# First stage of an adaLN transformer block: the blocks of normalized x transposed by a trip through memory and by VectorE

## The reference, cut to what matters

```python
# x (4, 1024, 1024) f32; wq (1024,1024), wk, wv (1024,256), wo (1024,1024); c (4,1024), wmod (1024, 6*1024)
mod = (_silu(c) @ wmod).reshape(4, 6, 1, -1)
sa, ca, ga, sb, cb, gb = (mod[:, n] for n in range(6))
ga, gb = (sign(g) * maximum(abs(g), 0.25) for g in (ga, gb))
h = _layernorm(x) * (1 + ca) + sa
q = h @ wq + bq; k = h @ wk + bk; v = h @ wv + bv      # 32 query heads, 8 key/value heads of 32
x = x + ga * (softmax(q k^T / sqrt(32)) v @ wo + bo)
h = _layernorm(x) * (1 + cb) + sb
x = x + gb * mixture_of_4_lora_experts(h)               # top 2 of 4, rank 16
```

## Time and profile before

| | us |
|---|---|
| median of 3 runs | 2806.36 (2805.2 to 2808.12) |
| the profiled execution, its own time | 2811.7 |
| its span | 2809.9 |
| block 1 / block 2 of the first stage | 69.64 / 74.06 |
| start of block 0's group 4 / of block 1 / of block 7 | 63.94 / 123.73 / 554.97 |

### The profile page before, as it was taken

One profiled execution on the slowest core, in us unless ns is written; L12 is line 12 of the kernel. 1 busy time (PEld: TensorE's weight loads), 2 busy tenths in 40 slices (PEclk: granted clock), 3 DMA queues, 4 the chain that ended last, 5 costly groups with the idle time before them and its releaser, 6 DMA issues.

```text
span 2809.9 us, 48988 instructions
## 1 busy us (share of the span) xinstructions
PE 2757.9 (98%) x14654; PEld 1701.5 (61%) x14654; DVE 2181.6 (78%) x2801; ACT 1529.6 (54%) x2963; POOL 1908.4 (68%) x710
## 2 busy tenths in 40 slices
PE   7999999999999999999999999999999999999998
PEld 4788888884444444444444444444444447888886
DVE  4433434348999999999999999999999968667665
ACT  3111111116776767777777776776767754545543
POOL 2433333317999999999999999999999985111110
PEclk9999999999999999999999999999999999999998
DMA  7544443434434344344444433444444443333231
GB/s 263 182 143 136 144 140 132 136 115 136 91 87 100 85 87 99 87 90 94 94 91 89 96 88 87 96 90 90 90 98 90 91 130 102 107 113 105 98 112 68
DMA packets 167501, 307.05 MB, mean 109 GB/s; under 512 B 49985, under 2 KB 91393, under 8 KB 159361
## 3 DMA queue, kind: packets, MB, share of 16 engines
q1 hardware_dynamic: 158352, 240.05, 29.3%
q0 software_dynamic: 9072, 66.06, 11.5%
HBM read 159.12 MB, written 79.82 MB: 85 GB/s over the span
## 4 chain that ended last, share of the span: by engine, by line
PE 74%; DVE 2%; ACT 1%; issue 1%; POOL 0%; DVEq 0%; ACTq 0%; POOLq 0%
PE back_ps L1348 21%; PE back_ps L1362 18%; PE s_ps L1322 16%; PE s_ps L1838 12%; PE back_ps L1887 2%; PE back_ps L1379 2%; PE back_ps L1859 1%; PE back_ps L1906 1%; DVE mx L1237 1%; PE back_ps L1337 0%; ACT h_t L1695 0%; PE s_ps L1411 0%; DVE a_lo L1281 0%; DVE xn L1753 0%; DVE two_sum L1252 0%
## 5 line engine op out<-in xcount | busy, mean ns | idle before, releaser
L1218 ACT ACTIVATE p_t<-back_ps 128x512 f32<-128x512 f32 x2048 | 1113.9, 596 | 432.0 <-PE back_ps L1348 390.2
L1237 DVE TENSOR_REDUCE mx<-s_ps 128x1 f32<-128x1024 f32 x1002 | 1172.3, 1208 | 84.4 <-PE s_ps L1322 76.8
L1128 POOL TENSOR_TENSOR p_sum<-p_sum,p_t 128x2048 f32<-128x2048 f32 x254 | 1166.3, 4592 | 23.0 <-ACT p_t L1218 6.5
L1348 PE MATMUL back_ps<-q_st,k_st 98*128 98x512 f32 x2048 | 812.5, 437 | 3.4 <-POOL ones L1097 2.4
L1348 PEld LDWEIGHTS back_ps<-q_st,k_st 98*128 98x128 f32 x2048 | 344.2, 188 | 593.8 <-ACT p_t L1218 496.4
L1322 PE MATMUL s_ps<-k_st,q_st 96*128 96x512 f32 x2004 | 629.3, 395 | 0.6 <-DVE mx L1237 0.4
L1362 PE MATMUL back_ps<-p_t,v_sb 128*32 128x512 f32 x4096 | 546.4, 605 | 0.0
L1322 PEld LDWEIGHTS s_ps<-k_st,q_st 96*128 96x128 f32 x2004 | 379.1, 189 | 70.6 <-DVE mx L1237 3.4
L574 POOL TENSOR_TENSOR o_lo<-side,o_hi 128x512 fp32r<-128x512 f32 x80 | 104.2, 1302 | 321.7 <-ACT o_hi L544 321.6
L1128 POOL TENSOR_TENSOR p_sum<-p_t 128x2048 f32<-128x2048 f32 x64 | 313.4, 4897 | 9.6 <-ACT p_t L1218 9.6
L1252 DVE TENSOR_REDUCE two_sum<-p_t 128x512 f32<-128x1024 f32 x256 | 317.8, 1243 | 0.9 <-ACT p_t L1218 0.9
(11 more groups left out here) (152 smaller groups left out, 2920.8 us busy)
## 6 DMA issues: line engine op xcount, KB each, us to landing
p_sum<-two_sum POOLq DMA_DIRECT2D x63, 1024.0 KB, 6.9
q_st<-q_hi_d SPq DMA_DIRECT2D x128, 256.0 KB, 4.3
stage<-w_mod SPq DMA_DIRECT2D x48, 512.0 KB, 6.2
q_hi_d<-o_hi SPq DMA_DIRECT2D x64, 256.0 KB, 2.0
q_lo_d<-o_lo SPq DMA_DIRECT2D x64, 256.0 KB, 2.0
q_st<-q_lo_d SPq DMA_DIRECT2D x64, 256.0 KB, 4.1
att_d<-a_sb SPq DMA_DIRECT2D x128, 128.0 KB, 2.3
a_f<-att_d SPq DMA_DIRECT2D x32, 512.0 KB, 4.7
```

The lines of the kernel that those rows point to most:

```text
L1128: nc.gpsimd.tensor_tensor(total, before, p_t[:, kt, :, :], ALU.add).then_inc(sum_done, 1)
L1218: nc.scalar.activation(p_t[:, s, c, :], st_ps[:, c % 2, :], ACT.Exp, scale=SCALE)\
L1237: nc.vector.tensor_reduce(mx[:, slot % 2, e:e + 1], s_ps[:, e % 2, :], AX_X, ALU.max)\
L1348: nc.tensor.matmul(st_ps[:, c % 2, :], k_st[:, slot // 2, s * P:(s + 1) * P], q_st[:, slot, jj, h * QW:(h + 1) * QW], start=True, stop=True)\
```

## The change

For all blocks but the first, PE no longer transposes normalized x. After `norm`, SP stores the half (256 rows, 1 MB) to an internal array `xn_d`, waits for its completion, and reads it back with four DMAs, one for each quarter of the partitions, such that every 32x32 square of the matrix lands where the transposed one belongs, each row of a square (32 floats, 128 bytes) being a piece of its own. The target `squares` is slots 2 and 3 of `stage`. In each turn DVE then transposes 128x256 elements in squares of 32 from `squares` into the PSUM bank that PE filled before, waits for that, and scales and shifts from there as before.

What follows from it: the slices of `w_mod` have two slots left, so `rows` and `mod` have four parts in place of two (the work of PE for each vector is the same); `fetch` waits for the store instead of for the transposes; the tables are moved: there are now about two groups between `norm` and the first turn.

```diff
     SLOTS = 4
+    MOD_SLOTS = 2
+    MOD_PARTS = KT // MOD_SLOTS
     MOD_CHUNKS = 2 * KT
...
-    PREPARE = {-1: [("fetch", 0)], 0: [("stats", 0)], 1: [("norm", 0)], 2: [("turn", 0, 0), ("turn", 0, 1)],
-               3: [("turn", 0, 2), ("turn", 0, 3)], 4: [("turn", 0, 4), ("turn", 0, 5)],
-               5: [("turn", 0, 6), ("turn", 0, 7), ("fetch", 1)], 7: [("stats", 1)], 8: [("norm", 1)],
-               9: [("turn", 1, 0), ("turn", 1, 1)], 10: [("turn", 1, 2), ("turn", 1, 3)],
+    PREPARE = {-1: [("fetch", 0)], 0: [("stats", 0)], 1: [("norm", 0)], 2: [("fetch", 1)],
+               3: [("turn", 0, 0), ("turn", 0, 1)], 4: [("turn", 0, 2), ("turn", 0, 3)],
+               5: [("turn", 0, 4), ("turn", 0, 5)], 6: [("turn", 0, 6), ("turn", 0, 7), ("stats", 1)],
+               7: [("norm", 1)], 9: [("turn", 1, 0), ("turn", 1, 1)], 10: [("turn", 1, 2), ("turn", 1, 3)],
                11: [("turn", 1, 4), ("turn", 1, 5)], 12: [("turn", 1, 6), ("turn", 1, 7)]}
-    MODULATE = {-1: [("rows", 0)], 3: [("mod", 0), ("rows", 1)], 11: [("mod", 1)]}
-
-
-    PREPARE_FIRST = {-1: [("fetch", 0)], 3: [("stats", 0)], 4: [("norm", 0)],
-                     5: [("turn", 0, 0), ("turn", 0, 1), ("turn", 0, 2)],
-                     6: [("turn", 0, 3), ("turn", 0, 4), ("turn", 0, 5)],
-                     7: [("turn", 0, 6), ("turn", 0, 7), ("fetch", 1)], 8: [("stats", 1)], 9: [("norm", 1)],
+    MODULATE = {-1: [("rows", 0)], 2: [("mod", 0), ("rows", 1)], 5: [("mod", 1), ("rows", 2)],
+                8: [("mod", 2), ("rows", 3)], 11: [("mod", 3)]}
+    PREPARE_FIRST = {-1: [("fetch", 0)], 3: [("stats", 0)], 4: [("norm", 0)], 5: [("fetch", 1)],
+                     6: [("turn", 0, 0), ("turn", 0, 1), ("turn", 0, 2)],
+                     7: [("turn", 0, 3), ("turn", 0, 4), ("turn", 0, 5)],
+                     8: [("turn", 0, 6), ("turn", 0, 7), ("stats", 1), ("norm", 1)],
                      10: [("turn", 1, 0), ("turn", 1, 1), ("turn", 1, 2)],
                      11: [("turn", 1, 3), ("turn", 1, 4), ("turn", 1, 5)],
                      12: [("turn", 1, 6), ("turn", 1, 7)]}
-    MODULATE_FIRST = {6: [("rows", 0)], 8: [("mod", 0), ("rows", 1)], 11: [("mod", 1)]}
+    MODULATE_FIRST = {5: [("rows", 0)], 7: [("mod", 0), ("rows", 1)], 9: [("mod", 1), ("rows", 2)],
+                      11: [("mod", 2), ("rows", 3)], 13: [("mod", 3)]}
     BESIDE_LAST = {-1: [("pairs",)], 12: [("negate",)], 13: [("scores", AHEAD - 2), ("scores", AHEAD - 1)]}
...
         xn = at("xn", [P, HT, D], F32, q_at + SLOTS * D * 4)
+        squares = stage[:, MOD_SLOTS:SLOTS, :].rearrange("p s (k n) -> p (s k) n", n=HALF)
         h_f = sb("h_f", [P, 2, HALF], F32)
...
                 def fetch(half):
-                    if not is_int(half, 0):
-                        sp.wait_ge(turned, half * KT)
+                    if is_int(half, 2):
+                        sp.wait_ge(turned, 2 * KT)
+                    elif not is_int(half, 0):
+                        sp.wait_ge(xn_out, half * 16 - 32)
                     sp.dma_start(xn[:, :, :], x[bass.ds(half * HALF, HALF), :].rearrange("(t p) d -> p t d", p=P))\
                       .then_inc(x_in, 16)
+                def turn_about(half):
+                    sp.wait_ge(xn_ready, half + 1)
+                    rows = xn_d[bass.ds(half * HALF, HALF), :]
+                    sp.dma_start(rows.rearrange("(t p) d -> p t d", p=P), xn[:, :, :]).then_inc(xn_out, 16)
+                    if is_int(half, 2):
+                        sp.wait_ge(wkv_lo_done, KT)
+                    sp.wait_ge(xn_out, half * 16 - 16)
+                    for n in range(4):
+                        src = rows.rearrange("(b t) (k n c) -> n t k b c", t=32, n=4, c=32)[n]
+                        sp.dma_start(squares[32 * n:32 * n + 32, :, :].rearrange("t k (b c) -> t k b c", c=32), src)\
+                          .then_inc(squares_in, 16)
                 sp.dma_start(cs[:, :, :], c_t).then_inc(small_in, 16)
...
                             fetch(i * 2 + (2 + ev[1]))
+                        elif ev[0] == "norm":
+                            turn_about(i * 2 + (2 + ev[1]))
                         elif ev[0] == "group" and ev[1] < QK:
...
                                 sp.wait_ge(wkv_lo_done, KT)
-                            sp.wait_ge(stage_used, vec * (2 * SLOTS) + (MOD_CHUNKS + ev[1] * SLOTS))
-                            for s in range(SLOTS):
+                            sp.wait_ge(stage_used, vec * KT + (MOD_CHUNKS + ev[1] * MOD_SLOTS))
+                            for s in range(MOD_SLOTS):
                                 sp.dma_start(stage[:, s, :],
-                                             w_mod_t[:, ev[1] * SLOTS + s, bass.ds(vec * D + 2 * D, D)])\
+                                             w_mod_t[:, ev[1] * MOD_SLOTS + s, bass.ds(vec * D + 2 * D, D)])\
                                   .then_inc(stage_in[s], 16)
-                        elif ev == ("mod", 1):
+                        elif ev == ("mod", MOD_PARTS - 1):
                             sp.wait_ge(row_ready, vec + 1)
...
                             bank = bank_at(i, hf, kt)
-                            dve.wait_ge(turned, tile + 1)
+                            source = t_ps[:, bank, 0:HALF]
+                            if is_int(i, -1):
+                                dve.wait_ge(turned, tile + 1)
+                            else:
+                                if kt == 0:
+                                    dve.wait_ge(squares_in, i * 128 + 64 * hf + 64)
+                                nc.vector.transpose(source, squares[:, kt, :]).then_inc(x_turned_done, 1)
+                                dve.wait_ge(x_turned_done, tile - 2 * KT + 1)
                             if not (is_int(i, -1) and kt == 0):
                                 dve.wait_ge(h_lo_done, tile - 1)
                             at = b + par
-                            nc.vector.tensor_scalar(h_f[:, bank, :], t_ps[:, bank, 0:HALF],
+                            nc.vector.tensor_scalar(h_f[:, bank, :], source,
                                                     scale1[:, kt, bass.ds(at, 1)], shift[:, kt, bass.ds(at, 1)],
...
                     for ev in evs:
-                        if ev[0] == "turn":
+                        if ev[0] == "turn" and not is_int(i, -1):
+                            pass
+                        elif ev[0] == "turn":
                             hf, kt = ev[1:]
...
                                 pe.wait_ge(row_ready, vec)
-                            for s in range(SLOTS):
-                                pe.wait_ge(stage_in[s], vec * 32 + (stage_base[s] + 16 * (part + 1)))
+                            for s in range(MOD_SLOTS):
+                                pe.wait_ge(stage_in[s], vec * (16 * MOD_PARTS) + (stage_base[s] + 16 * (part + 1)))
                                 for j in range(4):
                                     last = nc.tensor.matmul(m_ps[32 * j:32 * j + 32, 0:HALF],
-                                                            c_rep[:, part * SLOTS + s, :],
+                                                            c_rep[:, part * MOD_SLOTS + s, :],
                                                             stage[:, s, j * HALF:(j + 1) * HALF],
                                                             start=(part == 0 and s == 0),
-                                                            stop=(part == 1 and s == SLOTS - 1))
+                                                            stop=(part == MOD_PARTS - 1 and s == MOD_SLOTS - 1))
                                 last.then_inc(stage_used, 1)
```

More of the change, by code:

```diff
@@ L105, in adaln_block @@
     att_d = nc.dram_tensor("att_d", (NIT, P, S), F32, kind="Internal").ap()
+    xn_d = nc.dram_tensor("xn_d", (NTOK, D), F32, kind="Internal").ap()
     mod_raw_d = nc.dram_tensor("mod_raw_d", (4, NB, D), F32, kind="Internal").ap()
@@ L135, in adaln_block @@
         project(nc, x, w_q, w_k, w_v, b_q, b_k, b_v, c_t, w_mod, ident_in, ident,
-                q_hi_d, q_lo_d, k_hi_d, k_lo_d, v_d, mod_raw_d, mod_gate_d, ahead, q_at, k_at, m_at)
+                q_hi_d, q_lo_d, k_hi_d, k_lo_d, v_d, xn_d, mod_raw_d, mod_gate_d, ahead, q_at, k_at, m_at)
         wo_hi = keep("wo_hi", [P, KT, D], F32R)
@@ L193, in project @@
 def project(nc, x, w_q, w_k, w_v, b_q, b_k, b_v, c_t, w_mod, ident_in, ident,
-            q_hi_d, q_lo_d, k_hi_d, k_lo_d, v_d, mod_raw_d, mod_gate_d, ahead, q_at, k_at, m_at):
+            q_hi_d, q_lo_d, k_hi_d, k_lo_d, v_d, xn_d, mod_raw_d, mod_gate_d, ahead, q_at, k_at, m_at):
     NTOK, D = x.shape
@@ L360, in project @@
         turned = sem("turned")
+        xn_out = sem("xn_out")
+        squares_in = sem("squares_in")
+        x_turned_done = sem("x_turned_done")
         h_ready = sem("h_ready")
@@ L686, in do @@
                               .then_inc(ahead.m_lo_done, 1)
-                        elif ev == ("mod", 1):
```

(3 more changed lines are left out.)

## The result

The changed kernel took 2861.7 us (median of 4 runs, 2857.6 to 2871.7), the kernel before 2806.3: a ratio of 1.020, 95% interval 1.018 to 1.021. The forecast was 2847, range 2800 to 2905, slower with 0.83. The profiled execution is the slowest of its four: its span is 2870.0 us, against 2809.9 before.

The account below looks back on a forecast made before the run. PE, busy 98% of the span, was taken as the bound. Block 0 +17.4, odd blocks -0.3 and even blocks +8.7 gave 25.8 us, with the clock's 15 us 41: 2806.4 + 41 = 2847 us, range 2800 to 2905.

Parts of the forecast that it names:

- Block 0: First stage: `w_mod` queued behind the squares, PE waits 14.7 and 14.1 us, block 1 begins 17.4 us later.
- The trip: Each half's way through memory: store of 1 MB 5.3 us, four loads of 128-byte pieces 7.6 us.
- the nearer of the two readings: Squares' data time read from the store of v: 4.9 us at 216 GB/s, or 6.6 by packet time; 5.7 taken.
- Odd blocks: Blocks 1, 3, 5: late squares make PE wait 3.8 us, leaving about 0.1 of the 3.9 us gain.
- `w_mod` in four parts: Smaller `w_mod` parts in the first stage: some 0.5 us more PE time for each even block.
- Even blocks: Blocks 2, 4, 6: `w_mod` behind the squares, PE waits 2.3 and 4.0 us; loss 2.9 us a block.
- The clock: First stage: 1.5 us lost after each of 11 waits, less 1.5 in block 0: 15 us, bounds nothing to twice that.
- (a): Rival, chance 0.15: the squares' loads cost what 512-byte pieces do, 12.6 us; about 2925 us.
- (b): Rival, chance 0.05: DVE's transpose of 4-byte elements takes 1.23 us, 45 us more; about 2892 us.
- (c): Rival, chance 0.09: store and loads under 8.2 us, PE sets each block's end but for 0.7 us; 2777 us.
- (d): Rival, chance 0.08: steady blocks gain as with a short trip, block 0 loses its 17 us; about 2804 us.
- (e): Rival, no chance given: DVE's waits delay evacuations by over three groups and PE stalls; 4 to 5 us against 16.

Follow-up runs that it names:

- the kernel without a trip: Against the changed kernel: DVE transposes straight from normalized x, no store or loads, old preparation order, `w_mod` still in four parts, content wrong; 2801.9 us, 0.998 of before.
- the kernel with all three edits: Changed kernel with `w_mod` slices on ACT's queue, block 0 with PE's turns as before, and the second half's chain started earlier; 2792.8 us, 0.995 of before.

## Why the prediction was right, and where it missed

**Block 0** holds: waits of 14.7 and 14.1 us forecast, 13.9 and 14.1 measured, with `w_mod` behind the squares and `x`, as the sum had it. Of the 4.7 us above the 17.4 forecast some 4 are clock: PE is busy for 53.7 us in this block, against 49.6 in the kernel without a trip, which does the same work at clock 1.00.

**The trip.** Store 5.3 us forecast, 4.40 until SP went on (84.66 - 80.26); loads 7.6 forecast, 8.6 measured (93.28 - 84.66). The errors cancel, by luck. Over all 14 trips of the stage it is 11.9 to 14.0 us from the store's issue to the squares' use. The data rate was as in the nearer of the two readings of the earlier trace rows; much of the time is issuing, as this view of the DMA, 84 to 94 us in 40 slices, shows beside SP's 5.69 us for four loads:

```profile
GB/s 17 0 0 0 0 0 0 0 17 83 162 212 219 216 154 81 168 189 217 217 159 41 57 66 147 219 217 176 110 54 184 215 218 218 303 401 410 402 410 385
```

Each load has a plateau of 216 to 219 GB/s, and before the next one the rate falls to 81, 41 and 54: 256 KB at 218 GB/s take 1.2 us, an issue 5.69 / 4 = 1.42. But issuing is not all of it: in large pieces it took 3.9 us less, and the squares came 1.2 us sooner. The cost of packets in the Trainium skill ("DMA: Bandwidth & Descriptors", "Why small descriptors are slow (HBM only)") had given 4.6 us of data by estimate, 228 GB/s; the plateau agrees within 5%, but the time until the squares were there did not follow from it.

**DVE's transpose** holds: 0.42 us forecast, 0.45 measured. The group over 0 to 620 us:

```profile
L683 DVE STREAM_TRANSPOSE s_ps<-stage 128x256 f32<-128x256 f32 x112 | 50.5, 451 | 76.9 <-DMA stage<-xn_d 76.9
```

Two turns take 2.1 us, not 1.85, as this timeline of DVE at the end of block 1 shows (214.84 - 212.73):

```profile
212.73 0.46 DVE L683 STREAM_TRANSPOSE s_ps<-stage 128x256 f32<-128x256 f32 x1 [9.75 <-DMA stage<-xn_d]
213.33 0.54 DVE L690 TENSOR_SCALAR h_f<-s_ps,scale,shift 128x256 f32<-128x256 f32 x1
213.79 0.45 DVE L683 STREAM_TRANSPOSE s_ps<-stage 128x256 f32<-128x256 f32 x1
214.38 0.54 DVE L690 TENSOR_SCALAR h_f<-s_ps,scale,shift 128x256 f32<-128x256 f32 x1
214.84 0.41 DVE L707 TENSOR_TENSOR side<-o_ps,bias_v 128x256 f32<-128x256 f32 x1
```

**Odd blocks.** DVE waits 4.26 and 4.22 us for the second squares of blocks 3 and 5, forecast 4 to 5. PE waits 4.44 and 4.40 us at their end where 3.8 was forecast, and they take 0.9 us more than before where -0.1 was; 0.4 of that is PE's gain, 3.5 and not 3.9. Block 1 was missed: 9.9 us of waiting. The step that failed is that of `w_mod` in four parts, in which I counted PE's time and the arrival of the slices. I did not ask what the last part after group 13 sets free late: the eight row stores and behind them block 1's `fetch`. I followed SP's queue for the squares, and not for this part of `mod` that is moved too. With block 0 as before, block 1 takes 71.1 us and waits 5.0.

**Even blocks.** The wait before the last part was 5.9, 2.4 and 2.3 us, the forecast 4.0, and those before the second part at most 1.0 where 2.3 was forecast. The shape held: block 2 waits for `w_mod` and then 1.2 us for `h_lo`. The loss is 10.3, 6.0 and 7.9, as the clock stands at 0.50 for stretches up to 10 us. In block 2 the waits add up to 7.7, less 3.5 of turns plus 0.7 for four parts: 4.9. The stretch of 10.2 us at 0.50 has 6.22 us of busy PE, which is 3.1 us lost. The low stretch before it, from 217.70 to 227.90 with 4.37 us of busy PE, costs some 2 more, all of it in block 2.

**The clock.** By difference: 54.5 us, less 64.5 of waits, plus 24.5 of turns (7 x 3.5) and some 5 of waits in block 0 that went, less 2 for four parts, leaves about 18 us. PE's busy time says the same: 76.7, 74.8 and 77.4 us in the even blocks, against 71.2 for that work at clock 1.00, and 4 in block 0, are 19. That is within the bounds, nothing to 30, and above the 15 that I took.

**The rivals.** (a), loads at the price of 512-byte pieces, fell with the plateau of 218 GB/s; (b) with 0.45 us; (c) and (d) with the 13 us of the trip. (e) fell too: DVE waited up to 11.6 us for squares, and PE never for an evacuation. What I had not seen is that even a trip of no length would not have given (c)'s 2777: without any trip the kernel stands at 2801.9, since each block then ends with a wait of 1.1 to 2.4 us for `h_lo`, where (c) had 0.7, the turns save PE 3.5 us and not 3.9, and the clock falls after the longer of these waits.

So the forecast of 41 us more, where 55 came, is right in sign and by its mechanism: the waits of block 0, those of the even blocks, the chain that takes back the gain of the odd ones, and the clock. Of the missing 14 us, by the profile, block 1 is 6.6, the clock 3 to 4 and PE's gain, put 0.4 a block too high, 2.8.

## What to carry to other kernels

Work taken from the bounding engine is gained only up to the first limit beside it, and there may be several side by side. When taking away one wait brings little, take away two before concluding that the wait was not the cause. A transfer put on an in-order queue costs what stands behind it: list that first, both for the new transfer and for each step moved later, and move those to another queue before the change is judged. The engine that issues on the other queue has an in-order program as well: look what it waits for.

## What the runs showed of the hardware

- A DMA of 2048 pieces of 128 bytes kept SP for 1.42 us in the first trip, one in pieces of 8 KB for 0.44 (1.75 / 4). With 1.2 us of data each, issue sets the pace of four such in a row. I had counted nothing for it.
- In the rows above the scale and shift starts 0.60 and 0.59 us after the transpose that it needs, 0.14 after its end (over the stage 0.03 to 0.28 after it); from the scale and shift to the next, independent transpose it is nothing (213.33 to 213.79 for 0.54 us of work).
- In the kernel after, each of PE's eight waits of 2.3 to 14 us in this stage was followed by a stretch with the granted clock at 0.50 or 0.51; in the kernel with all three edits the clock was 1.00 in blocks 1 and 2, in spite of a wait of 1.46 us between them, while in the kernel before the 3 us after one of 1.44 us had 0.50.
